# Low parts of h in the second pair: from GpSimd to VectorE

## The reference

```python
x = L0_attn_x
xn = _layernorm(x, axis=-1)
s = _L0_attn_ref(xn, ...)
nx = xn * rsqrt(mean(xn * xn) + RMS_EPS) * ln_w
g = _silu(einsum('bsi,hi->bsh', silu(nx @ gate_w.T) * (nx @ up_w.T), down_w))
x = x + s * g
```

## Time and profile before

| | |
|---|---|
| median of 3 runs | 475.04 us (474.88 to 475.17) |
| the profiled execution's own time | 474.35 us |
| its span in the profile | 472.6 us |
| PE (matmul) busy | 466.3 us |
| VectorE (DVE) busy | 412.7 us |
| ScalarE (ACT) busy | 244.2 us |
| GpSimd (POOL) busy | 123.1 us |

### The profile page before, as it was taken

How to read it: one execution, slowest core, us unless ns; L and a number is a source line. 1 busy time by engine, 2 the same in 40 slices (tenths; PEclk the granted TensorE clock), 3 DMA queues, 4 the chain that set the end, 5 groups by cost and what they waited for, 6 DMA issues and landing times.

```text
span 472.6 us, 6217 instructions
## 1 busy us (share of the span) xinstructions
PE 466.3 (99%) x2122; PEld 391.0 (83%) x2122; DVE 412.7 (87%) x561; ACT 244.2 (52%) x417; POOL 123.1 (26%) x106
## 2 busy tenths in 40 slices
PE   7999999999999999999999999999999999999997
PEld 7898888888888888888888888888888888888886
DVE  6889778987898898889989898999998888888994
ACT  4785656658588888654122545225225335358102
POOL 5740312126222122233443101000011111126920
PEclk9999999999999999999999999999999999999999
DMA  8605996579779996573474649546556655514772
GB/s 269 252 2 225 345 380 262 234 259 273 205 248 301 298 360 255 188 268 133 135 235 162 218 187 371 202 184 223 222 201 223 223 200 200 201 44 135 276 259 89
DMA packets 44623, 105.70 MB, mean 224 GB/s; under 512 B 20272, under 2 KB 21808, under 8 KB 41264
## 3 DMA queue, kind: packets, MB, share of 16 engines
q1 hardware_dynamic: 44592, 105.31, 63.3%
HBM read 69.90 MB, written 35.40 MB: 223 GB/s over the span
## 4 chain that ended last, share of the span: by engine, by line
PE 95%; DVE 2%; DMA 1%; ACT 1%; SPq 0%; POOL 0%; issue 0%
PE gu_ps L553 18%; PE gu_ps L555 18%; PE gu_ps L556 18%; PE y_ps L687 8%; PE y_ps L688 8%; PE y_ps L689 8%; PE gu_ps L688 3%; PE gu_ps L687 3%; PE gu_ps L689 3%; PE gu_ps L718 2%; PE gu_ps L715 2%; PE gu_ps L714 2%; DMA xz<-x 1%; DVE w_ops L1166 1%; PE y_ps L727 0%; DVE stats L1075 0%
## 5 line engine op out<-in xcount | busy, mean ns | idle before, releaser
L553 PE MATMUL gu_ps<-z_hi,w_ops 128*128 128x512 f32 x378 | 147.2, 390 | 0.1
L556 PE MATMUL gu_ps<-z_hi,w_ops 128*128 128x512 f32 x378 | 147.1, 389 | 0.0
L555 PE MATMUL gu_ps<-z_lo,w_ops 128*128 128x512 f32 x378 | 147.1, 389 | 0.0
L498 POOL TENSOR_TENSOR h_lo<-h,h_hi 128x512 fp32r<-128x512 f32 x28 | 37.4, 1335 | 226.8 <-ACT h_hi L916 226.6
L553 PEld LDWEIGHTS gu_ps<-z_hi,w_ops 128*128 128x128 f32 x378 | 71.0, 188 | 15.5 <-issue 0.4
L556 PEld LDWEIGHTS gu_ps<-z_hi,w_ops 128*128 128x128 f32 x378 | 70.9, 188 | 14.8
L555 PEld LDWEIGHTS gu_ps<-z_lo,w_ops 128*128 128x128 f32 x378 | 70.9, 188 | 14.5
L687 PE MATMUL y_ps<-wd_ops,h_hi 128*128 128x512 f32 x168 | 65.6, 390 | 0.0
L689 PE MATMUL y_ps<-wd_ops,h_lo 128*128 128x512 f32 x168 | 65.5, 390 | 0.0
L688 PE MATMUL y_ps<-wd_ops,h_hi 128*128 128x512 f32 x168 | 65.5, 390 | 0.0
L916 ACT ACTIVATE h_hi<-h 128x512 fp32r<-128x512 f32 x28 | 17.6, 630 | 58.9 <-DVE h L1208 58.9
(11 more groups left out here) (139 smaller groups left out, 753.0 us busy)
## 6 DMA issues: line engine op xcount, KB each, us to landing
w_kept<-w_ops SPq DMA_DIRECT2D x13, 1792.0 KB, 6.2
w_ops<-w_kept SPq DMA_DIRECT2D x13, 1792.0 KB, 7.6
wd_ops<-wd_kept SPq DMA_DIRECT2D x35, 512.0 KB, 4.0
raw<-gate_up SPq DMA_DIRECT2D x30, 256.0 KB, 3.9
wd_kept<-wd_ops SPq DMA_DIRECT2D x14, 512.0 KB, 7.8
xz<-x SPq DMA_DIRECT2D x16, 256.0 KB, 5.3
raw<-down SPq DMA_DIRECT2D x14, 256.0 KB, 8.5
w_ops<-wd_kept SPq DMA_DIRECT2D x7, 512.0 KB, 7.5
```

The source lines that it names most:

```text
L498: pool.tensor_tensor(lo, src, hi.bitcast(F32), ALU.subtract).then_inc(h_lo_done, 1)
L553: pe.matmul(acc, w_h, z_hi[:, zi, c, :], start=start and c == 0, stop=False, skip_group_check=True)
L555: pe.matmul(acc, w_h, z_lo[:, zi, c, :], start=False, stop=False, skip_group_check=True)
L556: end = pe.matmul(acc, w_l, z_hi[:, zi, c, :], start=False, stop=c == 1, skip_group_check=True)
```

## The change

The low parts of items 28 to 55 are made by VectorE, with a semaphore of their own (h_lo_v_done), in place of GpSimd; those of items 0 to 27 stay. In groups 15 to 27 VectorE makes the low part of item g + 13 right behind c12(g - 1), ahead of its first steps of attention. Those of 41 and 42 stand ahead of c12(27), that of 43 ahead of times_up1(27), and those of 44 to 55 between steps of attention and finishes of block 2. GpSimd's queue ends with item 27. TensorE's wait ahead of a down product and ScalarE's wait ahead of silu0 look at the semaphore that belongs to the item.

```diff
+        h_lo_v_done = sem("h_lo_v_done")
...
+        def by_vector(u):
+
+            return u >= 2 * NI
+
+        def h_lo_count(u):
+
+            return u + 1 - 2 * NI if by_vector(u) else u + 1
...
                 pool.wait_ge(h_hi_done, u + 1)
-                if u < FREE:
-                    wait(pool, d_done, J * (u - 1))
+                wait(pool, d_done, J * (u - 1))
...
-            for u in range(NI, ITEMS):
+            for u in range(NI, 2 * NI):
                 h_lo_part(u)
...
             def down_wait(u):
-                pe.wait_ge(h_lo_done, u + 1)
+                pe.wait_ge(h_lo_v_done if by_vector(u) else h_lo_done, h_lo_count(u))
...
                 if g >= 2:
-                    act.wait_ge(h_lo_done, item_of((g - 2) // NI, 0, (g - 2) % NI) + 1)
+                    u = item_of((g - 2) // NI, 0, (g - 2) % NI)
+                    act.wait_ge(h_lo_v_done if by_vector(u) else h_lo_done, h_lo_count(u))
...
+            def h_lo_by_vector(u):
+                blk, n = item(u)
+                hi, lo = h_place(u)
+                dve.wait_ge(h_hi_done, u + 1)
+                if u < FREE:
+                    dve.wait_ge(d_done, J * (u - 1))
+                src = h_kept[:, n, :] if blk else h0[:, n % 2, :]
+                dve.tensor_tensor(lo, src, hi.bitcast(F32), ALU.subtract).then_inc(h_lo_v_done, 1)
...
             for g in range(NI, GROUPS):
                 if g > NI:
                     c12(g - 1)
+                    h_lo_by_vector(g + NI - 1)
                     attention(shares[g][0])
                     times_up1(g - 1)
...
+            h_lo_by_vector(2 * NI + NI - 1)
+            h_lo_by_vector(2 * NI + NI)
             c12(LAST)
+            h_lo_by_vector(FREE)
             times_up1(LAST)
-            attention(6)
-            for j in range(J):
-                finish(2, j)
-                attention(2)
+            for u, steps in enumerate((0, 1, 2, 2, 0, 0, 0, 0, 2, 2, 2, 2), FREE + 1):
+                h_lo_by_vector(u)
+                attention(steps)
+                if 0 <= u - FREE - 5 < J:
+                    finish(2, u - FREE - 5)
             attention(STEPS)
```

## The result

The changed kernel takes 475.9 us (median of 12 runs, 475.04 to 478.46), the kernel before 474.97 (12 runs, 474.19 to 475.31); the ratio is 1.0024, 95% interval 1.0013 to 1.0034. A second series of 11 runs gave 475.71 against 474.82, ratio 1.0019 (1.0010 to 1.0027). Both intervals leave out 1, so it is slower, by 0.9 us or 0.2%.

A forecast was written before the change was run, and what follows sets the result against it. PE was taken to bound the kernel, with no gap in the second pair. Nothing gained and stalls of 0.26 + 0.05 + 0.46 + 0.02 = 0.79 us lift the median from 475.04 to 475.8 us, range 475.3 to 476.6.

The forecast's parts named there:

- No gain for PE: Second pair: PE has no gap to close and isn't slowed by GpSimd, so taking GpSimd's work away gains nothing.
- The price of h_lo: VectorE: each low part runs 0.69 us and takes 0.61 us of the queue.
- the total 1.22: Sum of PE's stalls in us if each h_lo held VectorE's queue for 0.69; kernel time 476.3 us.
- Groups 18 to 21: VectorE's lateness builds up until ACT's seed is late and PE stalls 0.26 us before M6 of group 21.
- The carry: VectorE's starts carried forward through groups 18 to 21: 0.61, 0.96, 1.19, then 1.53 us late.
- 0.165 us: Delay from the end of what PE waits for to the equivalent start of PE's even stream.
- the term 0.26: PE's stall before M6 of group 21: seed ends at 345.13, wanted at 345.04, 0.26 us.
- The 0.05 in group 22: PE's stall before M6 of group 22: 0 to 0.2 us, taken as 0.05.
- Item 41: Start of the down product: 0.46 us stall for h_lo(41), then 0.02 for c12(27) at its third quarter.
- The tail: End of the kernel: nothing lost; attention ends near 460.9, about 0.8 us later, with 1.5 us to spare.
- The relief (9.0 us): Tail: VectorE's two-input operations no longer stretched by GpSimd's reads, 3.2 + 2.9 + 2.9 = 9.0 us.
- Sum: Whole kernel: 0.26 + 0.05 + 0.46 + 0.02 = 0.79 us slower, nothing gained; bounds 0.56 to 1.07.

The follow-up runs named there:

- gpsimd_six: Changed kernel with the low parts of items 31 to 34, 41 and 42 back on GpSimd; second pair 212.22 us, ratio to the kernel before 1.0004.
- all_mended: order_mended with one attention step moved from group 19 to group 16; second pair 212.23 us, ratio to the kernel before 1.0003.
- gpsimd_41: Changed kernel with only item 41's low part back on GpSimd; second pair 213.09 us, ratio to the kernel before 1.0015.
- gpsimd_41_42: Changed kernel with the low parts of items 41 and 42 back on GpSimd; second pair 212.62 us, ratio to the kernel before 1.0013.
- order_mended: Changed kernel with h_lo(41) moved behind c22(27), h_lo(42) behind c12(27), h_lo(43) behind times_up1(27); second pair 212.59 us, ratio to the kernel before 1.0008.
- twice: Changed kernel with the subtraction of items 31 to 34 made twice, once into an unread tile; second pair 215.45 us, ratio to the kernel before 1.0073.
- step_behind: Changed kernel with one attention step in each of groups 18 to 21 moved behind times_up1; second pair 213.71 us, ratio to the kernel before 1.0036.
- all_mended_13_26: all_mended with the low parts of items 13 and 26 on VectorE too; median 474.52 us, ratio to the kernel before 0.9992.

## Why the prediction was right

**No gain for PE.** Right: gpsimd_six and all_mended move 22 and 28 low parts off GpSimd and PE's stream is the same to 0.02 us. The relief shows on VectorE alone: 28 x 0.69 = 19.3 us of operations, 17.1 us of its queue, were added for 6.5 us of busy time.

**The price of h_lo.** 0.69 us and 0.61 of the queue: measured 680 ns on average in the tail, and 344.86 to 345.47 is 0.61. The sentence that the prediction set against it (the Trainium skill, VectorE: DVE Perf Modes, "The DRAIN you can't avoid") would have made it 0.69 and the total 1.22; these rows don't follow it. The prediction left out how that paragraph of the Trainium skill ends: "A next op that is not held starts earlier". So the section itself allows for what the rows show, though it gives no figure.

**Groups 18 to 21.** The carry's starts were met to 0.02 us. Mis-sized is only its last step: 0.165 us from the releaser's end to PE's even stream, taken from a wait for a low part, was 0.23 here (seed ended at 345.91; the stream runs as if restarted at 346.14). So the term 0.26 measured 0.35. The 0.05 in group 22 was nothing in this profile, and 0.03 in gpsimd_41, gpsimd_41_42 and order_mended. The two misses partly cancel. twice and step_behind show that the mechanism, not only its size, is right: the same carry, with the changed input, gave 3.3 to 3.4 and 1.5, and 3.24 and 1.50 were measured. The prediction named h_hi on ACT as what seed stands behind; in the trace silu1 starts 0.04 after c12's end, and h_hi ends within 0.03 of that, so VectorE's c12 is as much the limit.

**Item 41.** 0.46 + 0.02 forecast, 0.50 measured. The sum was right, but the text laid it at h_lo(41) alone. Its own numbers had c12(27) at 429.66 + 0.165 with a need at 429.82 that was already moved by the first stall; without that stall the need is 429.36 and c12 alone costs 0.46. gpsimd_41 shows it. Anyone who had mended "the" cause would have gained nothing.

**The tail.** Right that VectorE doesn't set the end, with the sum off by 0.9. Forecast: attention ends 0.8 later than before, 1.5 us spare. It ended at 460.75, 2.48 ahead of its user; less the 0.78 of the front that is 0.07 earlier than before. The relief (9.0 us) was there in full. The forecast counted h_lo(43) twice, once in the 13 x 0.61 and once in the 1.9 us by which times_up1(27) comes later, which makes 0.6; where the other 0.3 went was not taken apart.

**Sum.** 0.79 forecast, 0.86 measured in the trace, 0.93 and 0.89 in the medians.

## What to carry to other kernels

When the bounding engine has no gap, work taken off another engine can't help it, and each moved operation has to be placed by two dates: when the bounding engine wants it, and when the operations behind it in its new queue are wanted. An operation that waits for a third engine must not stand ahead of one whose inputs are there. And before moving a filler out of the way, ask what idle time it filled and which two dependent operations it kept apart: on a nearly full engine lateness is load less idle time, added up over the stages, and it costs nothing until the first reserve is used up and then nearly one for one (2.38 us for 2.44 in twice).

## What the runs showed of the hardware

A stall of PE costs a little more than the wait. After the wait at item 41 the second matmul starts 0.34 us behind the first, 0.11 more than the even 0.227, and the next ones 0.23 to 0.24 apart (429.81, 430.04, 430.28), which adds about 0.05 us over six of them.

In the profile of all_mended_13_26 PE's granted clock was at its lower level of 1.2 GHz for some 3.4 us in the front (worked out from the means), a mean of 0.73 and 0.93 of full speed in two stretches in which the kernel before had 1.00. PE had been idle for 1.2 of the 5 us ahead of them, where in the kernel before it was idle for 0.3. But that idle time doesn't explain it: the changed kernel's profile has 1.65 us of it in the same stretch, and 1.00 throughout. Nor does the 1.22 us pause right in front of the fall, at 12.15: at the same place PE stood idle for 1.40 in gpsimd_six and 1.70 in order_mended, at 1.00. Columns: stretch, PE busy (instructions), granted clock, DMA share, GB/s.

```profile
5.00:10.00 5.00, 3.81 (x28) 1.00 0.99 292
10.00:15.00 5.00, 3.78 (x14) 0.73 1.00 308
15.00:20.00 5.00, 5.00 (x22) 0.93 1.00 378
```

This execution started item 0's product at 50.34, the latest of all. It is one profile of thirteen, and what set the clock down is open; none of this kernel's edits lies that early. The timed runs have it too, in the kernel before as well: the mean granted clock was 0.992 in the changed kernel's slowest run (478.46 us), and 0.995 and 0.996 in the slowest runs of two series of the kernel before (476.13 and 475.83 us).
